# Twenty-three expert tiles instead of twenty-four, and raw key and value weights in the other buffer

## The reference

```python
router = xf @ gate_w.T                      # 2048 tokens, 8 experts
probs = softmax(router)
top_p, top_i = top_k(probs, 2)              # each token goes to two experts
combine = zeros((n, 8)).at[arange(n)[:, None], top_i].set(top_p)
h = silu(einsum('nc,efc->enf', xf, expert_fc1)) * einsum('nc,efc->enf', xf, expert_fc2)   # 352 wide
y = einsum('ne,enc->nc', combine, einsum('enf,ecf->enc', h, expert_proj))
y = y + sigmoid(xf @ shared_gate_w.T) * shared_expert(xf)                                 # 1408 wide
```

## Time and profile before

| | |
|---|---|
| time, median of 3 executions | 2285.54 us (2282.08 to 2286.4) |
| time of the profiled execution | 2289.88 us |
| its span, first to last instruction | 2288.1 us |
| mean granted TensorE clock | 0.995 |
| TensorE (PE) busy | 2230.0 us, 97% |
| VectorE (DVE) busy | 1432.6 us, 63% |
| ScalarE (ACT) busy | 1048.8 us, 46% |
| GpSimd (POOL) busy | 466.0 us, 20% |
| DMA | 222.33 MB, 97 GB/s over the span |

### The profile page before, as it was taken

How to read it: one execution, slowest core, us unless ns; L and a number is a source line. 1 busy time by engine, 2 the same in 40 slices (tenths; PEclk the granted TensorE clock), 3 DMA queues, 4 the chain that set the end, 5 groups by cost and what they waited for, 6 DMA issues and landing times. The chain is left out here.

```text
span 2288.1 us, 32149 instructions
## 1 busy us (share of the span) xinstructions
PE 2230.0 (97%) x11073; PEld 1852.4 (81%) x11073; DVE 1432.6 (63%) x2985; ACT 1048.8 (46%) x1870; POOL 466.0 (20%) x446
## 2 busy tenths in 40 slices
PE   7999999998999989999999999999998999999999
PEld 6777788887999977788888888888877888888887
DVE  6854365545777766767767677776776555555544
ACT  5532120103565556666666666666664322323221
POOL 4433545401111162000100001000032202121000
PEclk9999999999999999999999999999999999999999
DMA  6331321114877875101111000101102233232331
GB/s 223 127 106 43 107 64 28 33 58 161 286 280 266 274 274 205 43 19 38 37 29 35 28 28 28 37 18 37 34 4 79 80 105 102 97 126 72 111 115 51
DMA packets 92539, 222.33 MB, mean 97 GB/s; under 512 B 9616, under 2 KB 30608, under 8 KB 89360
## 3 DMA queue, kind: packets, MB, share of 16 engines
q1 hardware_dynamic: 84112, 193.65, 24.6%
q0 software_dynamic: 8320, 27.27, 4.7%
HBM read 176.85 MB, written 44.04 MB: 97 GB/s over the span
## 5 line engine op out<-in xcount | busy, mean ns | idle before, releaser
L2096 ACT ACTIVATE route_weights<-route_weights,xa_minus_max 128x512 f32<-128x512 f32 x256 | 184.8, 722 | 193.4 <-DVE xa_minus_max L2247 193.2
L2263 DVE TENSOR_TENSOR xa_late_hi<-xa_ps_t,route_wv_hi 128x512 fp32r<-128x512 f32 x256 | 174.9, 683 | 132.1 <-ACT route_wv_hi L2105 131.9
L2034 POOL TENSOR_TENSOR route_kv_lo<-route_rows,route_kv_hi 128x1024 fp32r<-128x1024 f32 x32 | 76.9, 2404 | 711.6 <-ACT route_kv_hi L2070 711.5
L2105 ACT ACTIVATE route_wv_hi<-xa_ps_t 128x512 fp32r<-128x512 f32 x256 | 151.4, 592 | 109.3 <-PE xa_ps_t L2450 72.1
L2247 DVE CUSTOM_DVE_ANT_0 route_weights<-xa_ps_s,route_mask_bias 128x512 f32<-128x512 f32 x256 | 175.6, 686 | 0.9 <-issue 0.6
L2450 PEld LDWEIGHTS xa_ps_t<-ident,route_weights 128*128 128x128 f32 x1024 | 126.6, 140 | 42.6 <-issue 9.8
L2450 PE MATMUL xa_ps_t<-ident,route_weights 128*128 128x128 f32 x1024 | 154.1, 273 | 5.0 <-DVE xa_late_hi L2263 5.0
L2822 ACT ACTIVATE ffn_silu<-ffn_ps_gate,late_scales 128x512 f32<-128x512 f32 x64 | 44.0, 688 | 248.9 <-PE ffn_ps_gate L86 248.9
L84 PE MATMUL xa_ps_p<-route_wv_hi,route_kv_hi 128*128 128x512 f32 x288 | 119.8, 416 | 8.1 <-ACT late_rows L2080 4.5
L2638 DVE TENSOR_TENSOR route_kv_lo<-route_weights,route_kv_hi 128x1024 fp32r<-128x1024 f32 x42 | 53.7, 1279 | 101.8 <-ACT route_kv_hi L2633 101.6
L1045 ACT ACTIVATE moe_silu<-moe_ps_gate 128x512 f32<-128x512 f32 x44 | 26.2, 596 | 197.2 <-PE moe_ps_gate L86 197.1
(11 more groups left out here) (535 smaller groups left out, 6642.1 us busy)
## 6 DMA issues: line engine op xcount, KB each, us to landing
route_weights<-in_ffn_w SPq DMA_DIRECT2D x64, 512.0 KB, 3.7
route_weights<-in_expert_w SPq DMA_DIRECT2D x12, 1408.0 KB
ex_w_raw<-in_expert_w SPq DMA_DIRECT2D x12, 1408.0 KB
route_weights<-wd_folded SPq DMA_DIRECT2D x64, 256.0 KB, 2.6
moe_y<-ex_y SPq DMA_DIRECT2D x40, 256.0 KB, 3.5
route_weights<-in_expert_w SPq DMA_DIRECT2D x12, 768.0 KB
ex_w_raw<-in_expert_w SPq DMA_DIRECT2D x12, 768.0 KB
route_weights<-in_xa_w SPq DMA_DIRECT2D x18, 512.0 KB, 3.6
```

Of the source, the lines that this page charges most:

```text
L2034: pool.tensor_tensor(kvl[b % 2][:], rawkv[b % 2], f32(kvh[b % 2][:]), ALU.subtract).then_inc(M.kv_ready, 1)
L2096: act.activation(prob[slot][:], prob[slot][:], ACT.Exp, bias=nmx[:, slot:slot + 1], scale=-1.0, accum_out=tot[:, slot:slot + 1]).then_inc( ...
L2105: act.activation(PTh[:, :, tt * P:(tt + 1) * P], psT[tt % 2][:].rearrange("p (k n) -> p k n", k=TT), ACT.Copy).then_inc(M.pt_hi, 1)
L2263: dve.tensor_tensor(PTl[:, :, tt * P:(tt + 1) * P], psT[tt % 2][:].rearrange("p (k n) -> p k n", k=TT), f32(PTh[:, :, tt * P:(tt + 1) * P] ...
```

## The change

The kernel holds 23 tiles: 16 large and 7 small (39 blocks; the table of slots keeps 40 columns). Where all 8 experts have an odd number of blocks, the last expert's odd block gets a large tile instead: `place_tiles` counts the odd experts and adds one large tile to expert 7, and cuts a negative count of small blocks to zero (5 more VectorE operations). The order of tiles is now large, large, large, large, small, then large, large, small as before: `Tile(0)` is dropped, `Tile(2)` becomes large, 5 tiles are written out ahead of the loop. Tile numbers `n` are shifted by one, so the parity of the last tile changes: it now uses `G.weights`, and the buffer that is free for the raw key and value weights is `w_raw1`. The wait for `M.wkv_ready` ahead of SP's `load_q` goes away. The roles of the two low-part activation buffers are swapped with it.

```diff
-BIGS, SMALLS = 2 * TOK // SLOTS, E
+BIGS, SMALLS = 2 * TOK // SLOTS, E - 1
 TILES = BIGS + SMALLS
 BLOCKS = SUBS * BIGS + SMALLS
+TABLE = BLOCKS + BLOCKS % 2
...
-                load_expert(sp, io, G, Tile(0), G.weights[:, 0:EW])
+                load_expert(sp, io, G, FIRST_TILE, G.weights[:, 0:EW])
...
                     big, small = nblock[:, 0, :], nblock[:, 1, :]
+                    odd, odds = load, sc1[:, 0:1]
+                    rt.link(dve.scalar_tensor_tensor(out=odd[:], in0=big, scalar=-float(SUBS), in1=small,
+                                                     op0=ALU.mult, op1=ALU.add))
+                    rt.link(dve.reduce_sum(odds, odd[:], axis=AX.X))
+                    rt.link(dve.tensor_scalar(odds, odds, SMALLS + 0.5, None, ALU.is_gt))
+                    rt.link(dve.tensor_tensor(big[:, E - 1:E], big[:, E - 1:E], odds, ALU.add))
                     before(start[:, 0, :], big)
...
+                    rt.link(dve.tensor_scalar(small, small, 0.0, None, ALU.max))
                     before(start[:, 1, :], small)
...
         r, q = divmod(j, 3)
+        opening = isinstance(it, int) and it == 0 and j < 3
         self.j, self.it = j, it
-        self.small, self.p = q == 2, j % 2
+        self.n, self.p = it * 6 + j - 1, (j - 1) % 2
+        self.small = q == 2 and not opening
...
+FIRST_TILE, LAST_TILE = Tile(1), Tile(TILES)
...
-        raw = [G.weights[:, 0:EW], sb("w_raw1", [P, EW], F32)]
+        raw = [sb("w_raw1", [P, EW], F32), G.weights[:, 0:EW]][::-1]
...
-        xl = [G.first_lo[:].rearrange("p (k n) -> p k n", k=KC), sb("xT_lo1", [P, KC, SLOTS], F32R)]
+        xl = [sb("xT_lo0", [P, KC, SLOTS], F32R), G.first_lo[:].rearrange("p (k n) -> p k n", k=KC)]
...
-            for j in range(Tile.ROUND):
-                body(Tile(j), "first" if j == 0 else "middle")
-            with eng.Fori(1, TILES // Tile.ROUND - 1) as it:
+            for j in range(1, Tile.ROUND):
+                body(Tile(j), "first" if j == 1 else "middle")
+            with eng.Fori(1, (TILES + 1) // Tile.ROUND - 1) as it:
...
-        LAST = Tile(TILES - 1)
+        LAST = LAST_TILE
+        G.raw_wkv = raw[1 - LAST.p]
...
-            sp.dma_start(G.weights[:, n * groups * D:(n + 1) * groups * D].rearrange("p (g d) -> p g d", g=groups),
+            sp.dma_start(G.raw_wkv[:, n * groups * D:(n + 1) * groups * D].rearrange("p (g d) -> p g d", g=groups),
...
                     load_context(sp, io, G, b, b % 2)
-                sp.wait_ge(M.wkv_ready, 2)
                 load_q(sp, io, G, 0)
```

More of the change, by code:

```diff
@@ L997, in _ @@
                     pool.wait_ge(xn_stored[i], 16 * (NT // XN))
-                for j in range(2):
-                    gather_rows(pool, G, Tile(j))
+                for t in (FIRST_TILE, FIRST_TILE.after(1)):
+                    gather_rows(pool, G, t)
             @block.scalar
@@ L1319, in fill_table @@
                     for t in range(NT):
-                        last = pe.matmul(psG[FILL_STEPS[k] % 2][:, 0:BLOCKS], at_low[t // HEAD][:, t % HEAD, :],
+                        last = pe.matmul(psG[FILL_STEPS[k] % 2][:, 0:TABLE], at_low[t // HEAD][:, t % HEAD, :],
                                          token_at[:, t, :], start=t == 0, stop=t == NT - 1)
@@ L1482, in steps @@
         def steps(eng, body):
-            for j in range(Tile.ROUND):
-                body(Tile(j), "first" if j == 0 else "middle")
-            with eng.Fori(1, TILES // Tile.ROUND - 1) as it:
+            for j in range(1, Tile.ROUND):
+                body(Tile(j), "first" if j == 1 else "middle")
+            with eng.Fori(1, (TILES + 1) // Tile.ROUND - 1) as it:
                 for j in range(Tile.ROUND):
                     body(Tile(j, it), "middle")
-            for j in range(TILES - Tile.ROUND, TILES):
-                body(Tile(j), "last" if j == TILES - 1 else "middle")
+            for j in range(TILES + 1 - Tile.ROUND, TILES + 1):
+                body(Tile(j), "last" if j == TILES else "middle")
         def chunk(buffer, f):
@@ L1516, in _ @@
             def _(sp):
-                load_expert(sp, io, G, Tile(1), raw[1])
+                load_expert(sp, io, G, FIRST_TILE.after(1), raw[1])
                 sp.dma_start(mask8[:], io["mask"].partition_broadcast(P)).then_inc(M.mask_loaded, 16)
@@ L1546, in _ @@
             def _(pool):
-                for j in range(2, TILES):
+                for j in range(3, TILES + 1):
                     pool.wait_ge(M.turned, Tile(j - 1).subs_before)
@@ L1736, in gate_up @@
                         ins.then_inc(M.h_done, 1)
-                turn(Tile(0))
+                turn(FIRST_TILE)
                 def body(t, which):
@@ L1772, in raw_values @@
 def raw_values(G):
-    return G.weights[:, KV * GROUPS * D:2 * KV * GROUPS * D]
+    return G.raw_wkv[:, KV * GROUPS * D:2 * KV * GROUPS * D]
 def value_half(w, half):
@@ L1831, in cross_attention @@
         HEAD = 2 * NW
-        rw = G.weights[:, 0:HEAD]
+        rw = G.raw_wkv
         rq, ro = G.weights[:, 0:NQ], G.weights[:, 0:NO]
```

43 lines of the change are left out of this document (23 added, 20 removed).

## The result

The changed kernel takes 2281.22 us (median of 7 executions, 2276.82 to 2282.7), the kernel before, timed beside it, 2285.92 us (7, 2282.08 to 2289.28). The ratio is 0.9967, with a 95% interval of 0.9955 to 0.9979: 7.5 us less, between 4.8 and 10.3. The profiled execution took 2282.07 us, its span is 2280.3 us, 7.8 less than before.

The account below looks back on a forecast made before the run. TensorE, busy 97% of the span, was taken to bound the kernel. The tile's -6.62, 0 for order and routing, and -0.7 for the handover gave -7.3 us: 2285.54 to 2278.2 us, range 2273.0 to 2282.5.

Parts of the forecast that it names:

- The removed tile: Expert stage: one small tile fewer saves its stretch of TensorE's time, start to start, -6.62 us.
- What else the tile had: Expert stage: the small tile's splits, load, gather, store and copy lie beside TensorE's work; removing them gives nothing.
- The new order: Start of the expert stage: the now large third tile's input is ready with 2.4 us to spare; cost 0.
- Rival 4: Expert stage: the third tile 3 us late, sum -4.3 us, 2281.2 us; chance 0.16 together with rival 2.
- The routing: Behind `place_tiles`: five more VectorE operations, 1.0 us, fit in a 2.63 us gap; cost on the path 0.
- The handover: Start of cross attention: the wait taken out of SP's queue lets loads and stores go earlier, -0.7 us.
- The copy of unit 5: Key and value units: its wait was to be about 1 us instead of 2.96 us.
- The wait at unit 13: Key and value units: TensorE's wait stays between 3.5 and 4.4 us, with the half clock still behind it.
- Rivals 1 to 3: Handover outcomes; the second: unit 4's landing 3 us later, -3.6 us, 2281.9 us, chance 0.16 together with Rival 4.
- rival 1: Handover gains much more: with the wait at unit 13 gone, -12.3 us, 2273.2; half of it, -9.5 us; chance 0.17.
- Rival 3: Slower: a store in the ring lands 8.4 us later, +1.8 us, up to +5.2 us, 2290.7; chance 0.05.
- The stretches at the low clock: Other stages: forecast called wrong if the shift alone puts a stretch there under the half clock; no size given.

Follow-up runs that it names:

- e3: The kernel before, with the query load and the two constants moved behind the store of unit 5: 2286.75 us, ratio 0.9997.
- e5: The changed kernel with the small tile before last left 1 matmul per PSUM bank for its 24 + 9 products, splits and loads kept: 2279.55 us, ratio 0.9979.
- e10: The changed kernel once more, nothing edited, timed beside the late-loads variant: 2279.46 us, ratio 0.9968.
- e0: The changed kernel once more, nothing edited, beside the variants on the same chip: 2281.21 us, ratio 0.9963.
- e9: The changed kernel with a ring of 8 stages for units 0 to 31 and query load, fourth context and constants behind units 5, 9, 14: 2276.83 us, 0.9970.
- e2: The changed kernel with query load, fourth context and two constants behind the stores of units 5, 9 and 14: 2278.6 us, ratio 0.9954.
- e8: The changed kernel without the products of the small tile before last, its weight splits also cut to 8 columns: 2279.03 us, one execution.
- e11: e2 run again beside the unedited changed kernel: 2279.62 us, ratio 0.9970.

## Why the prediction was right, point by point

Forecast: -7.3 us, 2278.2 us, between 2273.0 and 2282.5. Measured: 0.9967, or -7.5 us, and -7.3 us (0.9968) and -8.5 us (0.9963) when it was run again; medians 2281.22, 2281.21 and 2279.46. What the profiles account for is the tile, 6.7 us. The other 0.8 us of the 7.5 has no source that the runs show, and with an interval 5.5 us wide the agreement of 7.3 with 7.5 is in part luck.

- **The removed tile, -6.62 us:** right. -6.72 us between the only two kinds of profile: 263.10 with 24 tiles (before, e3), 256.36 to 256.39 with 23 in all ten that change nothing in that stretch. The rounds are 33.85 us as before. The 0.10 us that the four terms don't hold belong to the small tile as well: a large tile between large ones takes 13.57 us (568.36 to 581.93 above), so that a round has 33.85 - 2 x 13.57 = 6.71 us for its small one, not 6.62.
- **What else the tile had "gives nothing":** right as a sum, but for a reason that was too coarse. I measured VectorE's spare time over a round; e5 shows that beside the small tile, once its products are out, there is none to speak of: the products alone, with the splits left in, would have given 0.5 us.
- **The new order, 0:** right. Forecast in the time of the profile before, the third tile was to start at 565.4; the second starts 3.02 us later in the profile after, which makes 568.4, and it starts at 568.36 with no wait. Rival 4 is out.
- **The routing, 0 on the path:** right. The gap was to fall to about 1.6 us and is 1.42.
- **The handover, -0.7 us:** this is the term that the runs don't bear out as a gain. SP's queue did what was forecast: query weights 0.88 us behind the contexts, the first store 2.02 us sooner behind the first unit. But the idle DMA time that was to give the 0.7 us was not filled: the share is 0.91 over the same 7 us in both kernels. So the step from an earlier issue to a fuller DMA failed, and with it the reason for the gain. By the rule of the Trainium skill that the prediction drew on ("DMA: Bandwidth & Descriptors", section "Queues, rings and completion order") each DMA engine takes turns between the queues that it has work for; that a transfer moved forward takes its turns from others is worked out from it. The runs don't contradict this: in the pairs of kernels with the ring of 5, moving the query weights forward or back changed no time by more than the intervals can tell. The copy of unit 5 waited 2.45 us instead of the forecast 1 us. The wait at unit 13 was to be 3.5 to 4.4 us and was 1.57, 2.58 and 3.98 us in three profiles of the same code: one forecast from one profile of a wait that scatters by more than 2 us. The half clock that was to stand behind it was missing in the first and there in the other two. Taken over the profiles, the term is +0.5 us, with 1.5 and 3.8 us of scatter inside the two groups: not told apart from nothing, and not from -0.7 either.
- **Rivals 1 to 3:** the first profile, with 2.59 us less for the units, looked like rival 1; the same code at 89.08 and 90.02 us took that back. No kernel with 23 tiles was slower than before. Rival 3 is thereby out for the time, though not its mechanism: in e10 the wait for a landing was nearly as long as before.
- **The stretches at the low clock:** I wrote that the forecast is wrong if the shift alone puts another stretch there. It came and went in several places (below). So the condition was badly put: these stretches scatter between executions of one kernel, and the ratio, taken over several executions, came out as forecast.

The forecast for the median is 3.0 us under the first median and 1.3 us under that of 12 executions. The changed kernel's times lie in two heaps in the first seven, 2276.8 to 2277.1 and 2281.2 to 2282.7, so that the median of seven depends on which heap gets the fourth; the twelve of e10 fill the space between, 2277.4 to 2284.9.

## What to carry to other kernels

Where TensorE works without a wait, a piece of work that is removed on all engines at once is worth its length on TensorE's line from start to start, here to 0.1 us in 6.7. Removed on TensorE alone it may be worth a tenth of that: look at the other engines in the place, not over a round. Before a wait at a stage's start is explained from one profile, take two more of the same code; here they differed among themselves by more than the term that I was pricing.

## What the runs showed of the hardware

TensorE's clock falls to 1.2 GHz for stretches of 3.4 us, at some places 6.8 or 10.2 us, in places that differ between executions of the same code. (Windows cut exactly to such a stretch show 0.50; those printed here are cut a little off its edges and show 0.54 to 0.57.) One place is common to all profiles: the opening of the expert stage, 6.8 or 10.2 us. The two profiles with 24 tiles show what this does to the time: 23.9 us at half clock before, 13.7 us in e3, which by half of the difference is 5.1 us, and their spans are 2288.1 and 2283.0 us. For the changed kernel it is 20.5, 10.2 and 17.1 us with spans of 2280.3, 2275.8 and 2277.4 us (after, e0, e10), the same order but not the same size. Ahead of the expert stage the first turn comes at 528.1 to 529.6 us in the nine profiles with no such stretch, at 531.25 with one, at 531.5 and 531.75 with two, at 534.3 and 535.40 with three. At one boundary between groups of the shared expert TensorE waited 1.92 us in the profile after and 2.96 us in e9, and the clock fell; in the other twelve, e0 among them, it waited 1.11 to 1.25 us there and it didn't:

```profile
303.45 0.52 PE L85 MATMUL moe_ps_y<-moe_w_first_hi,moe_hidden_hi 128*128 128x512 f32 x1 [1.92 <-DVE moe_hidden_lo L1279]
```

```profile
304.30:307.70 3.40, 3.40 (x11) 2.62 (x10) 3.40 (x4) 1.46 (x2) 3.32 (x4) 0.57 0.11 47
```

```profile
301.01 0.50 PE L85 MATMUL moe_ps_y<-moe_w_first_hi,moe_hidden_hi 128*128 128x512 f32 x1 [1.11 <-DVE moe_hidden_lo L1279]
```

In the key and value units the clock fell beside each of the nine waits of 2.49 us or more, beside none of the waits of 1.0 to 1.9 us, and beside one of two of 2.10 and 2.17 us. But the length of the wait isn't the whole of it. Late in the kernel the same wait, 1.17 to 1.19 us, stands in all fourteen profiles. Before the change the clock fell behind it:

```profile
1687.24 0.38 PE L2450 MATMUL xa_ps_t<-ident,route_weights 128*128 128x128 f32 x1 [1.19 <-DVE xa_late_hi L2263]
```

```profile
1687.80:1691.20 3.40, 3.40 (x12) 2.73 (x11) 2.46 (x9) 3.30 (x6) 3.13 (x4) 0.57 0.00 0
```

and after it not:

```profile
1681.05 0.52 PE L2466 MATMUL xa_ps_t<-ident,route_weights 128*128 128x128 f32 x3 [1.19 <-DVE xa_late_hi L2279]
```

```profile
1681.10:1684.50 3.40, 3.40 (x17) 2.86 (x18) 2.98 (x11) 3.30 (x7) 2.71 (x3) 1.00 0.03 5
```

It fell there in e2, e8 and e11 too (in e9 some 40 us later), and the last column of the table has the price: 1384.5 to 1384.7 us with the stretch, 1382.9 to 1383.1 without, 1.6 us. The Trainium skill, "TensorE: Matmul & The Clock Gate", section "Terms", puts the loss at the time spent throttled times one minus the granted share; for 3.4 us at 0.50 that is an estimate of 1.7 us. The profiles agree, with 1.6 us. What decides whether it falls behind a wait of 1 to 2 us stays open.
